# A hybrid block on one core: the windows' values by transfers, a folded weight, a reordered prologue, and the probabilities' scaling moved from GpSimd to ScalarE

## What is computed

```
xn    = layernorm(x)*g + b
delta = softplus((xn @ w_xproj[:, :64]) @ w_dt + b_dt)      # 512 x 128
Bs,Cs = xn @ w_xproj[:, 64:128], xn @ w_xproj[:, 128:]      # 64 states
h_t   = exp(-delta*exp(A_log)) * h + (delta*xn)*Bs          # a scan over 512 tokens,
y_t   = sum_n(h_t*Cs)                                       # 128 channels x 64 states
ssm   = (y + x*D_ssm) @ w_ssm_out
q,k,v = x@wq, x@wk, x@wv                                    # 16 heads of 8, 4 key/value heads
attn  = softmax(q k / sqrt(8) + bias, blocks of 32 queries on windows of 96 keys) v @ wo
out   = x + .2*attn + .45*ssm + .15*silu(conv4(x)) + .2*(x@w_wm + .3*memory attention)
```

## Time and profile before

| what | value |
|---|---|
| median of 3 runs | 1187.52 us (1183.56 to 1188.54) |
| time of the profiled execution | 1187.0 us |
| its span, first to last instruction | 1185.2 us |
| busy: DVE, POOL, PE, ACT | 84%, 80%, 75%, 71% of the span |
| mean granted clock of TensorE | 0.838 of full speed |

### The profile page before, as it was taken

How to read it: one execution, slowest core, us unless ns; L and a number is a source line. 1 busy time by engine, 2 the same in 40 slices (tenths; PEclk the granted TensorE clock), 3 DMA queues, 4 the chain that set the end, 5 groups by cost and what they waited for, 6 DMA issues and landing times. The chain is left out here.

```text
span 1185.2 us, 19428 instructions
## 1 busy us (share of the span) xinstructions
PE 890.7 (75%) x4372; PEld 370.4 (31%) x4372; DVE 991.5 (84%) x2310; ACT 837.1 (71%) x2247; POOL 951.2 (80%) x667
## 2 busy tenths in 40 slices
PE   4467778687787877878787687877869687787776
PEld 2122334232332324322243223422324232333332
DVE  2598997799887996979969899688997899789992
ACT  4677875777667775687757877577875877657771
POOL 5378996799877996879869899597996799769882
PEclk9667998788797887978779888787898788798888
DMA  4845575566653775555755657464665566567640
GB/s 114 209 113 155 167 191 145 139 161 175 160 143 113 186 175 150 139 134 156 185 143 139 173 150 192 129 153 125 187 171 148 138 166 174 153 160 173 165 117 9
DMA packets 112230, 180.03 MB, mean 152 GB/s; under 512 B 17106, under 2 KB 28902, under 8 KB 112102
## 3 DMA queue, kind: packets, MB, share of 16 engines
q1 hardware_dynamic: 111814, 178.44, 58.1%
q10 hardware_dynamic: 288, 0.20, 0.1%
HBM read 171.18 MB, written 5.05 MB: 149 GB/s over the span
## 5 line engine op out<-in xcount | busy, mean ns | idle before, releaser
L1364 POOL TENSOR_TENSOR prod<-hst,C 128x1024 f32<-128x1024 f32 x256 | 602.5, 2356 | 178.7 <-DVE hst L1177 177.8
L1177 DVE TENSOR_TENSOR_SCAN hst<-decay,bank 128x512 f32<-128x512 f32 x384 | 459.7, 1208 | 23.7 <-POOL prod L1364 20.8
L1165 DVE TENSOR_TENSOR bank<-bank,B 128x512 f32<-128x512 f32 x384 | 262.1, 683 | 87.8 <-PE bank L911 41.8
L628 ACT ACTIVATE decay<-wide,A_rep 128x512 f32<-128x512 f32 x384 | 273.4, 714 | 43.1 <-DVE hst L1177 40.2
L878 PE MATMUL bank<-spread,sel_bc 96*128 96x512 bf16 x384 | 169.2, 442 | 153.4 <-DVE hst L1177 140.3
L642 ACT ACTIVATE prob<-s_sb,nmax 128x96 f32<-128x96 f32 x512 | 184.7, 363 | 0.8 <-DVE nmax L1190 0.3
L902 PE MATMUL bank<-prod,sel_red 128*32 128x512 f32 x1024 | 179.0, 779 | 7.9 <-POOL prod L1364 7.8
L1380 POOL TENSOR_TENSOR uwide<-uwide,B 128x512 f32<-128x512 f32 x128 | 163.0, 1273 | 23.6 <-DMA uwide<-u_rows 23.6
L1177 DVE TENSOR_TENSOR_SCAN hst<-bank,uwide 128x512 f32<-128x512 f32 x128 | 155.1, 1212 | 5.3 <-ACT bank L628 5.3
L911 PE MATMUL bank<-k,q 128*128 128x384 f32 x256 | 130.8, 598 | 12.3 <-DVE nmax L1190 12.0
L878 PEld LDWEIGHTS bank<-spread,sel_bc 96*128 96x128 bf16 x384 | 40.3, 105 | 306.6 <-DVE hst L1177 229.9
(11 more groups left out here) (185 smaller groups left out, 1072.5 us busy)
## 6 DMA issues: line engine op xcount, KB each, us to landing
wide<-dt_rows SPq DMA_DIRECT2D x512, 256.0 KB, 4.7
uwide<-u_rows SPq DMA_DIRECT2D x128, 256.0 KB, 4.1
spread<-parts SPq DMA_DIRECT2D x66, 32.0 KB, 3.4
x_sb<-in_L_attn_x_dram SPq DMA_DIRECT2D x8, 256.0 KB, 4.3
dt_rows<-sp_t SPq DMA_DIRECT2D x8, 256.0 KB, 3.9
out_dram<-outb SPq DMA_DIRECT2D x8, 256.0 KB, 4.5
bias<-rel_table SPq DMA_DIRECT2D x12, 48.0 KB, 1.9
u_rows<-uv SPq DMA_DIRECT2D x8, 64.0 KB, 3.6
```

Source lines behind the costliest of these rows:

```text
L628: nc.scalar.activation(to, wide[m % SLOTS][:, s % 2, :], ACT.Exp, scale=A_rep[:, g:g + 1]).then_inc(exp_done, 1)
L1165: v.tensor_tensor(uP[s % 4][:, :], uP[s % 4][:, :], B2[p][:, :], ALU.mult).then_inc(dbx_done, 1)
L1177: v.tensor_tensor_scan(hst[:, s % 4, :], kept, into[:, :], 0.0, ALU.mult, ALU.add).then_inc(scan_done, 1)
L1364: g.tensor_tensor(prod[:, 2 * (m % 4):2 * (m % 4) + 2, :], hst[:, 2 * (m % 2):2 * (m % 2) + 2, :], C2[p][:, :].unsqueeze(1).to_broadcast([ ...
```

## The change

1. **Values by transfers.** The job "v" does each 128-token tile once, in 4 matmuls; ACT copies it to `v_tok`, and SP issues 12 transfers (`window_values`, three in each of the unit pairs 0 to 3 of the batch) that put the windows together in `vw`. `values` of block 0 waits for them (`v_in`).
2. **Folded weights.** The job "dti" goes: a matmul and copies in the prologue form `w_delta = w_xproj[:, :64] @ w_dt`, and "dtpre" uses it. `y_start` goes: D_ssm*w_ssm is added to `w_x`, and the first `reduce_group` starts the sum.
3. **Softplus.** 1+exp is formed by ACT (`sp_t`), no longer by DVE (`softplus_sum`, L1135).
4. **Prologue and places.** In `front`, SP issues the later weights first, then the bias table's transfers (4 loads, not 12; DVE copies the other two tables in step 1); ACT does the layernorm before the decay rates, and the parts and first decays before the key copies. `project` starts in step 1 rather than 0, `y_copy` goes from step 2 to 5, and some jobs move by a step.
5. **Scaling of the probabilities.** `prob_norm` is four ACT instructions of 96 columns with a scale per partition, at lag 7; POOL's single instruction over 384 columns at lag 5 goes.

```
-PRE = {n: i for i, n in enumerate(["xaT", "xnT", "dti", "dtpre", "B", "C", "q", "k", "v"])}
+PRE = {n: i for i, n in enumerate(["xaT", "xnT", "dtpre", "B", "C", "q", "k", "v"])}
...
-    "reduce": 3, "y_copy": 2, "project": 0, "proj_copy": 11, "residual": 13, "aggr2": 15, "root2": 16,
-    "normalise2": 21, "ffn": 24, "output": 26,
...
+    "reduce": 3, "y_copy": 5, "project": 1, "proj_copy": 12, "residual": 14, "aggr2": 16, "root2": 17,
+    "normalise2": 20, "ffn": 25, "output": 27,
...
-BIAS_LAG, EXP_LAG, INV_LAG, NORM_LAG, PT_LAG, PT_COPY_LAG, PV_LAG, AO_COPY_LAG = 2, (3, 4), 6, 5, 9, 9, 11, 11
+BIAS_LAG, EXP_LAG, INV_LAG, NORM_LAG, PT_LAG, PT_COPY_LAG, PV_LAG, AO_COPY_LAG = 2, (3, 4), 6, 7, 9, 9, 11, 11
...
+                    if m in VALUE_DMA_AT and not first(B):
+                        window_values(B, VALUE_DMA_AT[m])
...
+            def window_values(B, which):
+
+                wait(sp, done["p"], job_count("p", B, "v"))
+                for j, m in (divmod(n, 4) for n in which):
+                    blocks = [n for n in range(NBLK) if 0 <= n - 1 + j < NBLK and (n - 1 + j) % 4 == m]
+                    t0 = (blocks[0] - 1 + j) // 4
+                    sp.dma_start(vw[32 * j:32 * j + 32, blocks[0]:blocks[-1] + 1:4, :, :]
+                                 .rearrange("p n g h -> p n (g h)"),
+                                 v_tok[32 * m:32 * m + 32, t0:t0 + len(blocks), :, :]
+                                 .rearrange("p t g h -> p t (g h)")).then_inc(v_in, 16)
...
             def front(B, p):
+                load_weights()
+                bias_out()
                 store_rows(B, p)
                 spread_parts(sp, B, p, 0)
                 widen(B, p, 0)
+                bias_back()
                 for m in range(1, SLOTS):
                     widen(B, p, m)
                 for m in range(U_SLOTS):
                     widen_u(B, p, m)
-                load_weights()
+                for at in VALUE_DMA_AT.values():
+                    window_values(B, at)
...
+                wait(act, sp_step, B * N_SP + SP["exp"])
+                nc.scalar.activation(sp_t[:, :], sp_e[:, :], ACT.Identity, bias=1.0).then_inc(sp_step, 1)
...
                     if name == "q":
                         high_parts(B)
+                        mid_parts(B)
+                        for part in (1, 2):
+                            spread_parts(act, B, p, part)
                         act.wait_ge(const_ready, 3)
                         act.wait_ge(head_tables, 3)
                     if name == "k":
-                        mid_parts(B)
+                        for s in range(AHEAD):
+                            unit_exp(B, s)
...
+            def prob_norm(B, k):
+                wait(act, p_inv, B * NBLK + k + 1)
+                for g in range(KVH):
+                    ins = nc.scalar.activation(prob[:, k % 4, g, :], prob[:, k % 4, g, :], ACT.Copy,
+                                               scale=pinv[:, k % 4, g:g + 1])
+                ins.then_inc(p_norm, 1)
...
-                    for n in range(NBLK):
-                        ins = mm(job[0:3 * W, n * 32:(n + 1) * 32], xaT[p][:, n * W:n * W + 3 * W], wv_s[:, :],
-                                 start=True, stop=True)
+                    for t in range(NT):
+                        ins = mm(job[:, t * 32:(t + 1) * 32], xaT[p][:, HALO + t * 128:HALO + (t + 1) * 128],
+                                 wv_s[:, :], start=True, stop=True)
...
+                if i == 0:
+                    wait(pe, y_evac, B)
...
-                    wait(pe, done["p"], job_count("p", B, "v"))
+                    wait(pe, v_in, (B + 1) * 16 * N_V_DMA)
...
+                dve.wait_ge(delta_weight, 1)
+                v.tensor_scalar(w_dtiT[:, :], bank[0][0:DTR, 0:D], 1.0, None, ALU.mult).then_inc(delta_weight, 1)
...
+                for row in (0, 2):
+                    v.tensor_scalar(bias3[:, row, :, W * (row == 0):3 * W - W * (row == 2)],
+                                    bias3[:, 1, :, W * (row == 0):3 * W - W * (row == 2)], 1.0, None, ALU.mult)
...
-            def prob_norm(B, k):
-                wait(pool, p_inv, B * NBLK + k + 1)
-                g.tensor_tensor(prob[:, k % 4, :, :], prob[:, k % 4, :, :],
-                                pinv[:, k % 4, :].unsqueeze(2).to_broadcast([128, KVH, 3 * W]), ALU.mult) \
-                    .then_inc(p_norm, 1)
```

## The result

The changed kernel takes 1239.95 us (median of 4 runs, 1238.3 to 1240.79), beside 1188.03 us for the kernel before on the same chip. The ratio is 1.0436, with a 95% interval from 1.0396 to 1.0476: 4.4% slower, where 1156 us was forecast. The profiled span is 1238.6 us, 53.4 more than before.

What follows compares the result with a forecast made beforehand. Bound by DVE's work, a bubble of some 9 us at batch starts made by PE, and smaller stalls. 1187.0 - 42 - 7.5 + 1.5 + 1.5 + 15 = 1155.5, so 1156 us; range 1100 to 1200.

Steps and rivals of the forecast that it cites:

- the middle of the bounds: Steady stretch of 105 us: between 99.7 and 114.6 us, taken as 106.9, +1.9 a batch, +15 in all.
- the second rival: Steady part: ACT becomes the bound and keeps its waits for PE; +77 instead of +15, 1218 us; chance 0.15.
- the term for ACT, DVE and POOL: Steady part: ACT's added scaling against DVE's saved waits, +15 us in all, extremes -43 and +77.
- The rival's own yardstick: ACT's waits for probT and ao: about 62 us means the middle, near 124 the second rival.
- The saving of 5.3 us a batch: Steady part: DVE's waits for POOL (20.8 us) and the softplus exponential (21.4 us) go, 5.3 us a batch.
- The boundary: Batch starts: shorter "v" and projection behind the scores bring scores 6.3 us sooner, 4 at batch 1; 42 us gained.
- that rival: Batch starts: the bubble mostly stays as key copies come later; only some 12 of 42 us gained, 1186; chance 0.12.
- The new wait: Block 0's `values` waits for the twelve transfers: 0.2 us a batch, 1.5 in all, between 0 and 2 a batch.
- what it could not see: Unseen effects, such as the twelve transfers crowding out `wide` loads; chance 0.05.
- The prologue: Before the first scans: u ready near 25 us, unit 3 scanned from about 44.5; 7.5 us gained, between 4 and 11.
- the weight's copy: Prologue, DVE: folded weight's first copy, if held beside POOL's memsets like `ddiag` (3.22 us), starts "dtpre" at 16.5.
- ACT's price for one scaling: Steady part, ACT: 0.27 us per instruction, 1.07 for four, 17 us a batch, 137 us in all.

Runs made afterwards that it cites:

- e8: Changed kernel with the scaling back on POOL at lag 5 and the feed-forward job with DVE's output put back to steps 24 to 26; 1144.19 us, ratio 0.965.
- e11: Changed kernel, scaling on ACT, with only the feed-forward job and DVE's output put back to steps 24 to 26; 1219.53 us, ratio 1.0277.
- e5: Changed kernel with scaling back on POOL and the moved residual-path, softplus and gate steps put back to their old places; 1150.56 us, ratio 0.9685.
- e7: Changed kernel with scaling back on POOL, and the values' windows again by 32 TensorE passes without transfers; 1184.86 us, ratio 0.9987.
- e4: Changed kernel with ACT's scaling issued behind the probT and ao copies of its step, not ahead of them; 1239.83 us, ratio 1.0455.
- e14: e11 with values and the copy of ao 10 steps behind the scores, not 11; 1220.37 us, ratio 1.0294.
- e9: e5 with the softplus and second layernorm early as in the change and the rounding left at step 24; 1158.31 us, ratio 0.9767.

## Why the prediction was wrong

**The term that failed** is the middle of the bounds: "If all waits vanish, the stretch takes 99.7 us, 5.3 less than now; if none does, 114.6, 9.6 more. No row tells where between. I take the middle, 106.9, +1.9 a batch and +15 in all." The stretch takes 115.5 us for 105.4, so +10.1 a batch: past the upper end, some +80 us over eight batches. That was the second rival ("ACT becomes the bound and keeps its waits"), which had a chance of 0.15 and a time of 1218. The same 48 units of batch 3 in e8 (scaling on POOL, feed-forward's place kept) and in e11 (the same with the scaling on ACT) tell what is in it (windows again from `uwide` issue to `uwide` issue):

```profile
465.89:567.56 101.67, 76.35 (x400) 31.32 (x399) 93.31 (x232) 80.77 (x229) 93.21 (x67) 0.86 0.62 167
500.28:611.16 110.88, 79.74 (x418) 34.05 (x416) 93.68 (x232) 96.25 (x289) 81.97 (x53) 0.86 0.56 151
```

The other parts of the change take 3.7 us off the stretch (105.4 to 101.7), the scaling puts 9.2 on, and the feed-forward's place 4.6 more (110.9 to 115.5; batch 3 has more than its share of this one). In whole kernels the same three are -42 (before to e8), +75 (e8 to e11) and +20 us (e11 to the changed kernel), which makes the 53. So the term for ACT, DVE and POOL was +15 and came to some +75, beside a term of 20 us that was missing.

That the measured 115.5 lies so near the bound of 114.6 is partly luck. The bound was ACT's busy time plus its waits for probT and ao: 99.1 + 15.5. Measured it is 95.9 + 12.5 = 108.4; it leaves out all other idle time of ACT, 7.2 us here and 11.2 us already in the kernel before, and takes its waits from the whole batch, where the stretch has 13.0. The reason given for shrinking waits, "an ACT that comes later finds PE done", was not so: ACT's two waits in the stretch stayed as they were, while PE's wait for ACT's copy of ao grew from 14.9 to 105.3 us in the whole, so PE comes later too. The rival's own yardstick misled: ACT's waits for probT and ao fell in the whole to 93.8 us, halfway between the forecast's 62 and the rival's 124; only read in the stretch do they say it.

**The saving of 5.3 us a batch** (DVE's waits for POOL and for the exponential) didn't come. The wait for the exponential went from the list and that for POOL fell from 20.8 to 6.5 us, but DVE, in order, met the next. In e5, with POOL scaling and places as before, the wait for the logarithm is 40.2 us; before, the waits for exponential and logarithm together were 31.6 + 5.5 = 37.1. That wait had only changed its name.

**A term was missing**: that moved jobs collide. The change moves the feed-forward behind a block's scores on PE, 20 us, and the prediction gave the moved steps no price. With part 5 undone and this place repaired (e8) the rest gives 42 us. The prediction's terms for boundary, prologue and what goes with them came to 46.5, but e8 holds the saving on the exponential as well, so this is not a check of each of them.

**The boundary** was right in its mechanism and too large in size: 5.0 us at the start of batch 3, not 6.3. "v" takes 1.92 us, not 1.33, so it gives 3.4; the projection ahead of the scores had held them for 1.7 (471.01 to 472.72), not 1.9; and the short waits between the matmuls did not shrink. The wait of 2.85 us for the key copies is unchanged, as said; so the bubble shrank, and that rival fell.

**The new wait** was small as forecast: PE waits 2.4 us in all for `vw`. The transfers do crowd out `wide` loads, which the prediction kept among what it could not see, but only once: in the prologue the twelve stand on SP from 39.65 to 47.8 us, ahead of the next `wide` loads, and ACT then waits for one.

```profile
39.65 8.16 SPq L452 DMA_DIRECT2D vw<-v_tok  x12
53.31 0.72 ACT L659 ACTIVATE decay<-wide,A_rep 128x512 f32<-128x512 f32 x1 [4.24 <-DMA wide<-dt_rows]
```

In e7, without the transfers, this wait is not there. DVE has table work until 57.7 us, so what it cost is open.

**The prologue** began as said, by two errors that cancelled, and then lost part of it:

```profile
12.75 0.62 DVE L1108 TENSOR_SCALAR w_delta<-bank 128x128 f32<-128x128 f32 x1
...
14.72 2.05 PE L892 MATMUL bank<-xnT,w_delta 128*128 128x512 f32 x2 [0.96 <-ACT xnT L586]
...
24.39 0.69 DVE L332 TENSOR_TENSOR uv<-sp_t,xnT 128x512 f32<-128x512 f32 x1
...
39.35 0.47 DVE L1115 TENSOR_SCALAR bias<-bias 128x256 f32<-128x256 f32 x2
...
45.25 1.26 POOL L1411 TENSOR_TENSOR uwide<-uwide,B 128x512 f32<-128x512 f32 x1 [21.43 <-DMA uwide<-u_rows]
...
52.50 0.40 DVE L1124 TENSOR_SCALAR wo_p<-wo_p 128x512 f32<-128x512 f32 x1
```

u ends at 25.1 us (said: 25.4), and the first scan starts at 38.2 (said: 35 to 38, and 38.4 by the 7.5 us of the sum). But "dtpre" starts at 14.72, not at 16.5. The 1.8 us gained are lost behind it: from "dtpre" to the end of u it takes 10.4 us, where the prediction carried over some 9. ACT's 1+exp now stands in this chain (0.63 us), and two of DVE's products (L332) take 1.08 us each instead of 0.69. SP's 18 weight loads end at 23.1 us, not 25.0. Then `uwide` of unit 3 came at 45.25 rather than 43, so unit 3 is scanned at 46.6 where 44.5 was said. The bias copies lie ahead of it, and the same table work in step 6 (`wo_p`) starts at 52.50 where it started at 56.68: 4.2 us left, where 6 were counted.

**On the weight's copy**: `ddiag` had taken 3.22 us beside POOL's memsets. The first copy, `w_dtiT`, stands in its place and takes 0.28 us; it was not held as `ddiag` was. The second can't tell. It stands behind a copy within SBUF, `wk_rep`, and both end as POOL's memset of `sel_bc` does, at 13.3 us:

```profile
11.28 0.28 DVE L1099 TENSOR_SCALAR w_dtiT<-bank 64x128 f32<-64x128 f32 x1 [6.27 <-PE bank L833]
11.48 1.80 POOL L1354 MEMSET sel_bc<- 96x2048 bf16 x1
11.68 1.68 DVE L1102 TENSOR_SCALAR wk_rep<-wk_s 128x128 f32<-128x128 f32 x1
```

So `wk_rep` reads as held, and `w_delta` (12.75 to 13.37, above) came out right behind it. By the rule of the Trainium skill (SBUF — State Buffer, Who interferes with whom), which the prediction weighed, a copy out of PSUM isn't held. `w_dtiT` does not contradict it, but it had started 0.2 us before the long memset, so it is weak evidence. On the other side the trace agrees: `cs_id`, within SBUF, took 1.28 us beside a POOL product of 1.31, and 0.21 us in the kernel before.

**ACT's price for one scaling** was nearly right: 362 ns each by the mean, 1.16 us for four, where 1.07 was taken, and 148 us in all, where 137 was.

```profile
L682 ACT ACTIVATE prob<-prob,pinv 128x96 f32<-128x96 f32 x512 | 148.3, 362 | 0.0
```

**What stays open**: the chain by which ACT's time reaches DVE. e4 rules out the order within the step. In e14 the wait moved to other instructions of ACT and the time stayed, which fits the sum of ACT's work and its alternation with PE, but e14 doesn't rule out the copy of ao, since its edit may cost what it gives. Taking that alternation away was not tried: it would need a further PSUM bank, and the kernel already uses all of the eight that it declares.

## What to carry to other kernels

Where two in-order engines alternate within a step, don't let added work on either eat the waits between them: here 148 us of instructions on an ACT that idled 23% of a stretch cost 56 to 75 us, net of what POOL was spared, and ACT's waits for PE in the stretch stayed. The second half of the work cost twice the first or more (50 to 25, 54 to 21 us), part of which may be POOL's relief. A wait that leaves the list of an in-order engine is no gain until the next wait in its order has been shown shorter, and its instructions no slower: in e9 the waits fell by 12 us and one instruction took back 10. And when jobs move by a step, look at what stands ahead of them in the new step on their own engine: one place of one job was 20 us. The better split was near at hand: with the scaling left on POOL and the feed-forward's place kept, the change makes 1142 to 1144 us, 3.5 to 3.8% faster than before.

## What the hardware showed unexpectedly

The "v" of 8 passes took 1.92 us, 0.24 each, and that of 32 passes 5.33, 0.167 each, both at the granted clock of 0.50, the lower of TensorE's two levels. The windows of the two jobs (columns as above), before:

```profile
462.30:467.60 5.30, 5.30 (x33) 5.22 (x33) 1.47 (x5) 0.69 (x1) 2.70 (x2) 0.50 0.79 202
```

and after:

```profile
483.80:485.80 2.00, 1.95 (x9) 1.81 (x9) 0.04 (x1) 0.72 (x1) 2.00 (x2) 0.50 0.72 210
```

Per pass the short job is dearer by 0.07 us. Its last pass's own length weighs more in a short group (0.40 us by the median, 0.35 in the old job), but that is the smaller part: without the last pass they follow each other every 0.22 us (1.52/7), against 0.16 (4.98/31). The new passes load weights of 128 columns, the old ones of 96, and their weight loads take 333 ns by the median against 280. The two spacings stand as 1.35 to 1, the columns as 1.33 to 1; that the columns are the reason was not measured by itself.

DVE's rounding is the other surprise: 0.69 us alone and 2.4 to 2.8 us beside a POOL product of 2.4, with both of its inputs in SBUF (e9, above). Moving a step of DVE by one place can so change how long it runs.
